# Gate weights side by side, both halves of y asked for at once, and router tokens that stand, in a four-layer kernel

## The reference, cut to what matters

```
# third layer; x here is the output of its mixing block, 2048 x 1024
base_out   = x @ base_w.T + base_b
res_hidden = x @ A.T                      # 64 numbers a token
logits     = x @ router_w.T               # 16 experts
probs      = softmax(logits); topw, topi = top_k(probs, 2)
combine    = one-hot rows of topi weighted by topw / (sum topw + 1e-6)
out        = base_out + 0.5 * einsum('bse,bsr,eor->bso', combine, res_hidden, B)

# fourth layer; hidden_states (y) is the output of its mixing block
logits     = y @ gate_w                   # 1024 x 8
routing    = top_k(logits, 2)
shared_out = relu(y @ up_w)**2 @ down_w   # 1024 x 2048, 2048 x 1024
routed_out = ((y @ fc1_w @ expert_w) * sum(routing)) @ fc2_w
out        = layernorm(shared_out + routed_out) * gamma + beta
x          = x + out
```

## Time and profile before

| | us |
|---|---|
| median of 3 runs | 1837.94 |
| lowest and highest | 1833.31, 1841.68 |
| the profiled execution | 1837.11 |
| span of its trace | 1835.3 |
| TensorE busy in it | 1717.5 |
| ScalarE, VectorE, GpSimd busy | 459.5, 823.1, 339.9 |

### The profile page before, as it was taken

One profiled execution on the slowest core, in us unless ns is written; L12 is line 12 of the kernel. 1 busy time (PEld: TensorE's weight loads), 2 busy tenths in 40 slices (PEclk: granted clock), 3 DMA queues, 4 the chain that ended last, 5 costly groups with the idle time before them and its releaser, 6 DMA issues.

```text
span 1835.3 us, 22240 instructions
## 1 busy us (share of the span) xinstructions
PE 1717.5 (94%) x8396; PEld 1409.7 (77%) x8396; DVE 823.1 (45%) x1453; ACT 459.5 (25%) x694; POOL 339.9 (19%) x186
## 2 busy tenths in 40 slices
PE   7899837989889999999999999999999999999997
PEld 3578726878678888888768888888777888888876
DVE  4256579995534334433323333333272333333326
ACT  2344323433311111111122222221223222222212
POOL 1100011234223333333221111111201111111110
PEclk9999968999999999999999999999999999999999
DMA  8277414567633233323661111111192111111114
GB/s 311 93 185 187 134 43 139 165 202 233 213 110 94 96 107 119 94 95 108 174 195 46 47 58 56 46 46 46 66 358 75 52 46 46 46 46 46 46 58 161
DMA packets 126803, 205.80 MB, mean 112 GB/s; under 512 B 14436, under 2 KB 82092, under 8 KB 126124
## 3 DMA queue, kind: packets, MB, share of 16 engines
q1 hardware_dynamic: 109428, 154.21, 26.8%
q0 software_dynamic: 11264, 27.27, 4.6%
q10 hardware_dynamic: 6048, 23.46, 3.8%
HBM read 143.01 MB, written 61.89 MB: 112 GB/s over the span
## 4 chain that ended last, share of the span: by engine, by line
PE 72%; DVE 7%; DMA 5%; SPq 1%; issue 1%; ACT 1%; POOL 0%; DVEq 0%; ACTq 0%
PE pd L1414 24%; PE pu L1414 23%; PE l_po L1414 18%; PE pf L1414 2%; DMA scratch_x<-l_x 2%; PE l_py L1388 1%; PE l_pr L1372 1%; DVE row_peak L838 1%; DMA l_base_lo<-scratch_y_lo 1%; SPq L446 1%; DMA X<-scratch_x 1%; DMA scratch_y_lo<-y_out_lo 1%; PE l_pc L1338 1%; DVE y1T L863 1%; ACT row_mag L790 1%
## 5 line engine op out<-in xcount | busy, mean ns | idle before, releaser
L1414 PE MATMUL pd<-down_hi,hid_hi 128*128 128x512 f32 x640 | 249.1, 389 | 2.9 <-issue 2.9
L1414 PE MATMUL pu<-l_base_hi,up_hi 128*128 128x512 f32 x640 | 249.2, 389 | 0.0
L1414 PE MATMUL pu<-l_base_lo,up_hi 128*128 128x512 f32 x640 | 249.0, 389 | 0.0
L1414 PE MATMUL pd<-down_hi,hid_lo 128*128 128x512 f32 x640 | 249.0, 389 | 0.0
L1414 PE MATMUL pd<-down_lo,hid_hi 128*128 128x512 f32 x640 | 249.0, 389 | 0.0
L1414 PE MATMUL pu<-l_base_hi,up_lo 128*128 128x512 f32 x640 | 249.0, 389 | 0.0
L1537 POOL TENSOR_TENSOR down_lo<-raw,down_hi 128x1024 fp32r<-128x1024 f32 x40 | 100.3, 2508 | 701.1 <-ACT down_hi L1550 701.1
L1702 DVE TENSOR_TENSOR hid_lo<-hidden,hid_hi 128x512 fp32r<-128x512 f32 x64 | 44.8, 700 | 395.8 <-ACT hid_hi L1611 395.8
L1642 DVE TENSOR_TENSOR acc<-pd,acc 128x512 f32<-128x512 f32 x224 | 143.6, 685 | 54.8 <-PE pd L1414 51.5
L1605 ACT ACTIVATE hidden<-pu 128x512 f32<-128x512 f32 x64 | 38.3, 598 | 462.4 <-PE pu L1414 462.4
L1414 PEld LDWEIGHTS pd<-down_hi,hid_hi 128*128 128x128 f32 x640 | 120.1, 188 | 28.7 <-issue 3.7
(11 more groups left out here) (244 smaller groups left out, 2841.4 us busy)
## 6 DMA issues: line engine op xcount, KB each, us to landing
X<-scratch_x SPq DMA_DIRECT2D x256, 64.0 KB, 2.7
l_x<-scratch_x SPq DMA_DIRECT2D x32, 512.0 KB, 4.6
raw<-in_up SPq DMA_DIRECT2D x32, 512.0 KB, 3.6
raw<-in_down SPq DMA_DIRECT2D x32, 512.0 KB, 4.3
x_in<-in_x SPq DMA_DIRECT2D x16, 512.0 KB, 4.2
scratch_x<-x_in SPq DMA_DIRECT2D x16, 512.0 KB, 3.9
scratch_x<-l_x SPq DMA_DIRECT2D x16, 512.0 KB, 5.7
scratch_y2T<-y2T SPq DMA_DIRECT2D x16, 512.0 KB, 3.0
```

Of the source, the lines that this page charges most:

```text
L1414: mm = pe.matmul(out, lhs[a], rhs[b], start=first and n == 0, stop=last and n == len(pairs) - 1)
```

## The change

Four edits are made.

1. Router: `y2`, the 128 tokens, is now the stationary operand and `war`'s 80 columns move. The result stands as 128 x 80 at once, in the banks `pr[0]` and `pr[1]` by turns. The copy to `rT` on ScalarE and the transposition on TensorE are gone, with their waits; VectorE waits for the product itself.
2. Gate: the high and low parts of the gate weights lie side by side in one tile of 16 columns. A chunk is two products, high y by 16 columns and low y by the 8 high columns, in place of three. The copy takes 16 rows, and the turning is a plain fp32 product with `sel`, two 8 x 8 unit matrices one above the other, which sums the two parts; VectorE makes `sel` once.
3. GpSimd issues the load of block 1 of y right behind that of block 0; the wait for tile 14's store is gone.
4. `up_hi` of `raw[1]` moves on ScalarE to before the cast of tile 15's y, behind a wait for the last expert product (`o_mm`).

```diff
@@ l3_buffers
-    names["eps"] = s_.sb("eps", [P, 16])
+    names["eps"], names["sel"] = s_.sb("eps", [P, 16]), s_.sb("gate_sel", [P, EG])
@@ phase_l2, gpsimd
                 pool.wait_ge(y3_stored, 32 * (NT // 2 + 1))
                 first["y"](pool, 0)
+                first["y"](pool, 1)
...
-            if isinstance(s, int) and s == NT:
-                pool.wait_ge(y3_stored, 32 * NT)
-                first["y"](pool, 1)
@@ phase_l2, scalar
-            if has[0]:
-                act.wait_ge(r_mm, s + 1)
-                act.copy(rT[:], pr[0][0:R2 + E2, 0:P]).then_inc(r_out, 1)
...
                 first["up_hi"](act, 0)
+                act.wait_ge(o_mm, 2 * NT + 4)
+                first["up_hi"](act, 1)
@@ phase_l2, vector
-                dve.wait_ge(r_turned, s + 1)
-                dve.tensor_copy(lg, pr[1][:, R2:R2 + E2]).then_inc(step, 1)
+                dve.wait_ge(r_mm, s + 1)
+                dve.tensor_copy(lg, pr[u][:, R2:R2 + E2]).then_inc(step, 1)
@@ phase_l2, tensor
-                    last = pe.matmul(pr[0][0:R2 + E2, 0:P], war[:, k, :], y2[:, k * P:(k + 1) * P],
+                    last = pe.matmul(pr[u][:, 0:R2 + E2], y2[:, k * P:(k + 1) * P], war[:, k, :],
                                      start=k == 0, stop=k == KC - 1)
...
-            if has[0]:
-                pe.wait_ge(r_out, s + 1)
-                if later(s, 1):
-                    pe.wait_ge(step, MS * (s - 1) + 2)
-                pe.transpose(pr[1][:, 0:R2 + E2], rT[:], K["ident"][0:R2 + E2, 0:R2 + E2]).then_inc(r_turned, 1)
@@ phase_l3
-        first_up_hi(act, 1)
...
-                act.copy(gT[:, n * HALF:(n + 1) * HALF], pd[n][0][0:EG, :]).then_inc(gT_made, 1)
+                act.copy(gT[:, n * HALF:(n + 1) * HALF], pd[n][0][0:2 * EG, :]).then_inc(gT_made, 1)
...
+        dve.tensor_tensor(sel, K["ident"][0:2 * EG, 0:EG], K["ident"][0:2 * EG, EG:2 * EG], ALU.add).then_inc(sel_made, 1)
...
                 for k in range(KC):
-                    last = split_product(pe, pd[n][0][0:EG, :], [w[:, k, :] for w in gate],
-                                         [v[:, k, n * HALF:(n + 1) * HALF] for v in y], k == 0, k == KC - 1)
+                    pe.matmul(pd[n][0][0:2 * EG, :], gate[:, k, :], y[0][:, k, cols], start=k == 0, stop=False)
+                    last = pe.matmul(pd[n][0][0:EG, :], gate[:, k, 0:EG], y[1][:, k, cols], start=False, stop=k == KC - 1)
...
+                pe.wait_ge(sel_made, 1)
                 for t in range(HT):
-                    last = pe.transpose(pd[0][1][:, t * EG:(t + 1) * EG], gT[:, t * P:(t + 1) * P], K["ident"][0:EG, 0:EG])
+                    last = pe.matmul(pd[0][1][:, t * EG:(t + 1) * EG], gT[:, t * P:(t + 1) * P], sel, start=True, stop=True)
```

More of the change, by code:

```diff
@@ L1024, in l2_buffers @@
     names["y2"] = s_.sb("l2_y2", [P, D])
-    names["war"], names["rT"] = s_.sb("l2_war", [P, KC, R2 + E2]), s_.sb("rT", [R2 + E2, P])
+    names["war"] = s_.sb("l2_war", [P, KC, R2 + E2])
     names["sm"], names["res"] = s_.sb("l2_small", [P, 8, E2]), s_.sb("l2_res", [P, R2])
-    s_.sb("l2_pad", [P, SMALL - KC * (R2 + E2) - P - 8 * E2 - R2])
+    s_.sb("l2_pad", [P, SMALL - KC * (R2 + E2) - 8 * E2 - R2])
     names["crT"] = s_.split("crT", [P, D])
@@ L1060, in phase_l2 @@
 def phase_l2(nc, K, A, SC, s_, buf, first, prior):
-    y3s, y3, x3b, x3, crT, war, mats, low, bias3, y2, y2s, x2, bias, beta, cr, rT, sm, res, pr, pc, po, py = [buf[n] for n in (
-        "y3s y3 x3b x3 crT war mats low bias3 y2 y2s x2 bias beta cr rT sm res pr pc po py").split()]
+    y3s, y3, x3b, x3, crT, war, mats, low, bias3, y2, y2s, x2, bias, beta, cr, sm, res, pr, pc, po, py = [buf[n] for n in (
+        "y3s y3 x3b x3 crT war mats low bias3 y2 y2s x2 bias beta cr sm res pr pc po py").split()]
     base = K["l2_base"]
@@ L1078, in phase_l2 @@
         "l2_y_loaded low_hi low_lo y2_hi y2_lo base_mm crT_lo gate_hi gate_lo")
-    (bias_loaded, beta_loaded, x_free, r_mm, r_out, r_turned, step, e_done, cr_made, cr_turned, crT_made, o_mm, xb,
+    (bias_loaded, beta_loaded, x_free, r_mm, step, e_done, cr_made, cr_turned, crT_made, o_mm, xb,
      x3_made, x3b_made, y_mm, y3_made, y3_hi, y3_lo) = s_.sems(
-        "l2_bias_loaded beta_loaded l2_x_read r_mm r_out r_turned mix_step exp_done cr_made cr_turned crT_made l2_o_mm "
+        "l2_bias_loaded beta_loaded l2_x_read r_mm mix_step exp_done cr_made cr_turned crT_made l2_o_mm "
         "l2_xb_made x3_made x3b_made y3_mm y3_made y3_hi y3_lo")
@@ L1185, in scalar @@
         act.wait_ge(K["l2_loaded"], 16)
-        act.copy(K["gate_s"][0][:], K["gate"][:]).then_inc(gate_hi, 1)
+        act.copy(K["gate_s"][:, :, 0:EG], K["gate"][:]).then_inc(gate_hi, 1)
         def low_high(k0, k1):
@@ L1207, in body @@
                     act.copy(crT[0][:, h * HALF:(h + 1) * HALF], pc[h][:]).then_inc(crT_made, 1)
[L1208 to L1210 removed]
             if not later(s, 1):
+                act.wait_ge(r_mm, 1)
                 act.wait_ge(y2_lo, 1)
@@ L1242, in vector @@
         dve.wait_ge(gate_hi, 1)
-        dve.tensor_tensor(K["gate_s"][1][:], K["gate"][:], K["gate_s"][0][:].bitcast(F32), ALU.subtract).then_inc(gate_lo, 1)
+        dve.tensor_tensor(K["gate_s"][:, :, EG:2 * EG], K["gate"][:], K["gate_s"][:, :, 0:EG].bitcast(F32), ALU.subtract).then_inc(gate_lo, 1)
         dve.wait_ge(gate_lo, 1)
@@ L1274, in body @@
                 at = MS * s
-                dve.wait_ge(r_turned, s + 1)
-                dve.tensor_copy(lg, pr[1][:, R2:R2 + E2]).then_inc(step, 1)
+                dve.wait_ge(r_mm, s + 1)
+                dve.tensor_copy(lg, pr[u][:, R2:R2 + E2]).then_inc(step, 1)
                 if later(s, 1):
                     dve.wait_ge(cr_made, s)
-                dve.tensor_copy(res[:], pr[1][:, 0:R2]).then_inc(step, 1)
+                dve.tensor_copy(res[:], pr[u][:, 0:R2]).then_inc(step, 1)
                 dve.wait_ge(step, at + 2)
@@ L1368, in body @@
                 pe.wait_ge(y_loaded, 16 * (s + 1))
-                if later(s, 1):
-                    pe.wait_ge(r_out, s)
+                if later(s, 2):
+                    pe.wait_ge(step, MS * (s - 2) + 2)
                 for k in range(KC):
-                    last = pe.matmul(pr[0][0:R2 + E2, 0:P], war[:, k, :], y2[:, k * P:(k + 1) * P],
+                    last = pe.matmul(pr[u][:, 0:R2 + E2], y2[:, k * P:(k + 1) * P], war[:, k, :],
                                      start=k == 0, stop=k == KC - 1)
@@ L1429, in phase_l3 @@
     y, gate, eps = K["l2_base"], K["gate_s"], buf["eps"]
-    gT = scratch[0:EG, :]
+    gT, sel = scratch[0:2 * EG, :], buf["sel"][0:2 * EG, :]
     pu = [pu_all[:, q * HALF:(q + 1) * HALF] for q in range(2 * NB)]
@@ L1436, in phase_l3 @@
         "up_hi up_lo down_hi down_lo up_mm relu squared hid_hi hid_lo down_mm added")
-    g_mm, gT_made, g_turned, g_out, topped, g_summed = s_.sems(
-        "gate_mm gateT_made gate_turned gate_out gate_topped gate_summed")
+    g_mm, gT_made, g_turned, g_out, topped, g_summed, sel_made = s_.sems(
+        "gate_mm gateT_made gate_turned gate_out gate_topped gate_summed gate_sel_made")
     gamma_loaded, eps_set, centred, ssq_made, rooted, inverted, weighed, out_made = s_.sems(
@@ L1816, in build @@
                  gate=s.sb("gate", [P, KC, EG]))
-        K["gate_s"] = s.split("gate", [P, KC, EG])
+        K["gate_s"] = s.sb("gate_pair", [P, KC, 2 * EG], F32R)
         with ExitStack() as shared:
```

1 line of the change is left out of this document (added).

## The result

| | before | changed |
|---|---|---|
| median (12 runs each) | 1838.17 us | 1829.22 us |
| lowest and highest | 1832.56, 1841.68 | 1821.22, 1832.44 |
| profiled execution | 1837.11 | 1830.79 |
| span of its trace | 1835.3 | 1828.9 |

The ratio is 0.995, with a 95% interval from 0.9935 to 0.9965: 9 us faster. The forecast was 1825.9 us, a gain of 11.2 us, with a range from 1815 to 1834.

A forecast was written before the change was run, and what follows sets the result against it. TensorE carries nearly all of the chain, except at the seam, where tile 14's store and block 1's load stand in it. Terms -1.0 (turning of `rT`), -2.6 (second half's gate) and -7.6 (seam) sum to -11.2: 1825.9 us, range 1815 to 1834.

The forecast's parts named there:

- rival C: Seam: T stays at 941.6 because SyncE's queue runs no sooner; -4.6 us at the seam, 1828.9 us in all; chance 0.18.
- T: Seam: landing of the first `down` chunk that ScalarE waits for; 941.64 before, forecast 938.5, bounds 937 and 941.6.
- The router product: Third layer: 16 instructions keep about 1.75 us a tile, since the 128-column weight load sets the pace; no change taken.
- The turning of `rT`: Third layer: transposition of the router result leaves the chain, 0.07 us in each of 14 tiles, -1.0 us.
- Sum -2.6: Second half's gate: 16 products fewer give -3.8 us, the dearer turning +1.2; range -3.2 to -2.5.
- The seam: Between third and fourth layers: early load of block 1 lets g = 1 begin at 949.4, not 956.97; -7.6 us.
- rival E: Seam: loads of y so quick that block 1 never holds TensorE; seam -9.1 us, 1824.4 us in all; chance 0.05.
- rival D: Seam: tile 14's store, starved by 8 MB of loads, delays ScalarE and T; +6.5 us, 1843.6 in all; chance 0.05.
- T + 9.6: Seam: when the weights for g = 1 are ready after T, through casts, low parts and load; forecast 948.1.
- I let the last 1.5 double: Seam: tile 14's store slows only in its last 1.5 us, beside block 1's load, landing at 918.2.
- costs nothing: Seam, ScalarE: early `up_hi` runs at about 908.5 while ScalarE waits; some 2.4 us possible delay covered by the store wait.
- B: Third layer's router product: moving columns set the pace, 0.64 us less in 14 tiles; 1816.2 us in all; chance 0.12.

## Why the forecast was right, and where it was off

**The direction and the main term were right.** Taking block 1's load off the chain was worth 6 us of the traces' 7, and undoing that edit alone gives it back (464.5 us for 458.6 in the traces, 5.1 us of the 9 by the ratios). The total alone doesn't show this: the measured 1829.2 us stands nearer to rival C's 1828.9 than to the forecast's 1825.9. The trace decides it, with T at 936.9 and not at 941.6. The nearness to C is chance.

**The router product: right.** 1.74 us for 16, set by the load; the split into 40 columns shows it. The step that argued from the setup's product of 128 loaded and 32 moving columns holds. That this product ran at 1.2 GHz is inferred from its pace, twice the 109 ns: the trace has no record of the granted clock before 32 us. The turning of `rT` was worth 0.12 us a tile (0.09 in the two versions with the gate of before) for the 0.07 taken from its row; the 48 products behind it are 0.07 shorter as well.

**The gate of the second half: the step "Sum -2.6" failed.** It measured +0.7. The term for 16 products fewer is right (7.56 us for 32 with the gate alone). The turning was sized right as well, 1.88 us for the 1.76 forecast. Missing was what it does to the work behind it, +1.6 us. The other 1.6 us are the gate's own cold start: 9.1 us for 32 in the changed kernel. The forecast took full clock after 1.92 us idle from the earlier trace rows. That row told of one execution: behind the same 1.9 us idle the gate started cold, 1.6 us slower, in five of the twelve traces, with the change's gate (three of six) and with the old one (two of six). The clock fell within the gate's first five products, 0.1 to 1.1 us after its start. With such counts I take it for luck and not for a cost of the change. The Trainium skill ("TensorE: Matmul & The Clock Gate", "What's actually happening") states that the number of products on the low clock varies from run to run. These traces, one execution of each version, fit that: seven gates with none, five with eight.

**The seam: -6.2 for -7.6.** Taken step by step from the last `l_py`:
- Gate(0) took 6.6 us for the 5.3 forecast: the clock rose only at 920. Stated as "at most 6.0", that bound was too tight.
- Block 1 landed at 928.1 for the 932.5 forecast, below the lower bound of 931.5. The four loads took 32.8 us in all, not the 35.4 of the second half. TensorE never waited for it, which is rival E's first half; the 1.2 us of wait in the sum went.
- Tile 14's store landed at 922.9, 20.9 us after its issue, for the 918.2 forecast. That is the starving of rival D, its sign "above 20 us", but short of the point of 926 that D names. D's sum is off by 1.3 us: it goes by T + 9.6, the weights' path, where the forecast's own path of copy, turning and q3 gives T + 10.9. With that, D stands at 968.4 for 967.1, and decides from a store landed at 924.7, so that the store came within 2 us of it. "I let the last 1.5 double" was too mild. T nevertheless came at 936.9 for 938.5, since what follows the store was quicker than I took it: in the kernel before SyncE's queue stood 6.61 us in the issue of gamma, with block 1's load under way, and in the changed kernel 0.94. The rows (SyncE's timeline, before and changed; the six traces with the late load have 6.48 to 6.76 us here, the other six 0.94 to 1.84):

```profile
926.90 6.61 SPq L1492 DMA_DIRECT2D gamma<-in_L_ffn_ln_gamma  x1
...
928.12 0.94 SPq L1485 DMA_DIRECT2D gamma<-in_L_ffn_ln_gamma  x1
```

- gate(1), q1 and the turning: 3.7, 5.4 and 1.9, as forecast.
- q3 took 7.1 us for 5.5: the fall of the clock, +1.6.

So two misses that cost (gate(0) +1.3, the clock +1.6) stand against waits of 1.5 us that weren't there.

**Edit 4, "costs nothing": right for the cost, too small for the worth.** It is worth 1.4 us in the traces, as a balance (above), and 2.0 by the ratios, whose intervals overlap. The forecast had seen `up_lo` take 5.83 us for 1.22 in the late place, with q2 as its user, and looked only at what the early place meets (3.35 us there, covered). It did not price the late place once block 1's wait no longer hides it.

**The rivals.** B is excluded by the split router. C did not come: T moved with SyncE's queue. D came half way. E was half right and cost nothing more, since gate(0) and the clock took up the time.

The medians moved by 9.0 us, the stretches of the two traces by 7.1 and the two profiled executions by 6.3: the changed one lay 1.6 us over its median, the other 1.1 under. Differences of this size are within the spread of single executions.

## What to carry to other kernels

When a TensorE instruction changes its kind, price what runs behind it too: 16 short products cost 1.3 us by their own row and, where the clock fell behind them, 1.6 us more, and putting the sum on VectorE beside a transposition won both back. Where few columns move, count stationary columns, not moving ones, when asking what a swapped operand order brings. And a single trace's clock at a short wait is one draw; price a cold start by its chance and not by the row that happened to be warm.
